# FFN coefficients broadcast in halves, the first during the second route, and half of F2's preparation in B's output path

## What is computed

```python
x = x + attn_a(layernorm(x))   # distances on a hyperboloid, 16 heads of 8
x = x + ffn(layernorm(x))      # "F1"
x = x + attn_b(layernorm(x))   # rotary softmax attention, 16 heads of 8; "B"
x = x + ffn(layernorm(x))      # "F2", the same weights as F1
```

```python
scores = sigmoid(x @ router_w.T)
sfc = scores + e_bias                      # choice only
group_scores = top_k(sfc by 8 groups, 2).sum   # best 4 groups stay
topk_idx = top_k(masked sfc, 8)
coef = scores of the chosen / their sum * 2.5, else 0    # (T, 64)
h = silu(x @ Wg[e]) * (x @ Wu[e]) * coef[:, e]           # all 64 experts
out = sum_e h @ Wd[e] + silu(x @ SWg) * (x @ SWu) @ SWd
```

## Time and profile before

| what | value |
|---|---|
| runs | 1180.27, 1181.67, 1187.24 us; median 1181.67 |
| profiled execution | 1185.19 us, span 1183.4 us |
| mean granted TensorE clock | 0.818 |
| PE busy | 982.2 us (83%), 5292 matmuls |
| DVE busy | 988.9 us (84%) |
| ACT, POOL busy | 693.6 us (59%), 343.4 us (29%) |
| DMA | 85.13 MB, mean 72 GB/s |
| F1's expert phase | about 392 to 666 us of the span |
| B | about 666 to 855 |
| F2's preparation and experts | about 855 to 1184 |

### The profile page before, as it was taken

How to read it: one execution, slowest core, us unless ns; L and a number is a source line. 1 busy time by engine, 2 the same in 40 slices (tenths; PEclk the granted TensorE clock), 3 DMA queues, 4 the chain that set the end, 5 groups by cost and what they waited for, 6 DMA issues and landing times.

```text
span 1183.4 us, 16824 instructions
## 1 busy us (share of the span) xinstructions
PE 982.2 (83%) x5292; PEld 712.1 (60%) x5292; DVE 988.9 (84%) x1489; ACT 693.6 (59%) x792; POOL 343.4 (29%) x215
## 2 busy tenths in 40 slices
PE   4774677766675899999999788999646999999997
PEld 3442344434443688888888546554534888888886
DVE  5649888888888699999999788996366999999996
ACT  2435999999994444455445451677253455445543
POOL 2003566555560142333332130100001333323320
PEclk8765555555556899999999895999957999999999
DMA  2000000000010697667663000000004987666651
GB/s 53 1 1 1 1 1 1 1 1 1 1 34 10 153 208 161 151 143 163 151 150 78 0 1 1 2 2 1 8 7 105 208 169 163 149 151 157 142 115 35
DMA packets 26236, 85.13 MB, mean 72 GB/s; under 512 B 3920, under 2 KB 17232, under 8 KB 18000
## 3 DMA queue, kind: packets, MB, share of 16 engines
q1 hardware_dynamic: 26192, 84.56, 32.1%
HBM read 82.45 MB, written 2.10 MB: 71 GB/s over the span
## 4 chain that ended last, share of the span: by engine, by line
PE 63%; DVE 22%; issue 9%; ACT 3%; DMA 2%; POOL 1%; SPq 0%; DVEq 0%; POOLq 0%; ACTq 0%
PE ps L445 60%; DVE xr L1682 4%; DVE xr L1674 3%; DVE mx L1824 3%; DVE stats L1442 1%; DVE rr L1690 1%; POOL rr L1344 1%; DVE hl L1915 1%; PE ps L507 1%; PE ps L832 1%; DMA cbc<-routing_coefficients 1%; DVE q L1853 1%; DVE mr L1585 1%; ACT f_xn L1172 1%; DMA routing_coefficients<-cT 0%
## 5 line engine op out<-in xcount | busy, mean ns | idle before, releaser
L1240 ACT ACTIVATE sg<-ps 128x512 f32<-128x512 f32 x264 | 156.8, 595 | 263.5 <-PE ps L445 263.5
L1908 DVE TENSOR_TENSOR hf<-sg,ps 128x512 f32<-128x512 f32 x264 | 172.6, 686 | 41.8 <-DVE hl L1915 23.6
L445 PE MATMUL ps<-xh,whi 128*128 128x512 f32 x528 | 206.3, 391 | 1.3 <-POOL wlo L1394 1.3
L445 PE MATMUL ps<-xh,wlo 128*128 128x512 f32 x528 | 205.5, 389 | 0.0
L445 PE MATMUL ps<-xl,whi 128*128 128x512 f32 x528 | 205.5, 389 | 0.0
L1344 POOL TENSOR_TENSOR rr<-xr,rr 128x2048 f32<-128x2048 f32 x32 | 144.9, 4546 | 193.3 <-ACT xr L1067 179.2
L1915 DVE TENSOR_TENSOR hl<-hf,hh 128x1024 fp32r<-128x1024 f32 x132 | 179.3, 1358 | 0.5 <-DVE hf L1908 0.5
L1392 POOL CAST whi<-wraw 128x384 fp32r<-128x384 f32 x66 | 53.9, 817 | 403.2 <-PE ps L445 267.4
L1920 DVE TENSOR_TENSOR hf<-hf,cbc 128x1024 f32<-128x1024 f32 x128 | 157.5, 1231 | 10.4 <-DMA cbc<-routing_coefficients 1.7
L1246 ACT ACTIVATE hh<-hf 128x1024 fp32r<-128x1024 f32 x132 | 139.0, 1053 | 5.0 <-DVE hf L1920 5.0
L1394 POOL TENSOR_TENSOR wlo<-wraw,whi 128x384 fp32r<-128x384 f32 x66 | 116.1, 1759 | 5.3
(11 more groups left out here) (251 smaller groups left out, 1597.1 us busy)
## 6 DMA issues: line engine op xcount, KB each, us to landing
cbc<-routing_coefficients SPq DMA_DIRECT2D x128, 512.0 KB, 6.3
wraw<-in_wexp_dram SPq DMA_DIRECT2D x66, 192.0 KB, 5.4
X<-in_x_dram SPq DMA_DIRECT2D x4, 256.0 KB, 4.5
routing_coefficients<-cT SPq DMA_DIRECT2D x8, 128.0 KB, 2.3
out_dram<-X SPq DMA_DIRECT2D x4, 256.0 KB, 2.9
rope_in<-in_consts_dram SPq DMA_DIRECT2D x1, 512.0 KB, 3.4
wa<-in_wA_dram SPq DMA_DIRECT2D x1, 256.0 KB, 3.8
w_in<-in_wB_dram SPq DMA_DIRECT2D x1, 128.0 KB, 3.2
```

The source lines that it names most:

```text
L445: return pe.matmul(o, l, r, start=start, stop=stop, **kw)
L1240: act.activation(sg[c % 2][:, :], bank(4 + 2 * (c % 2)), ACT.Silu).then_inc(s_sg, 1)
L1908: dve.tensor_tensor(hf[c // 2][:, c % 2 * FF_TOK:(c % 2 + 1) * FF_TOK], sg[c % 2][:, :], bank(5 + 2 * (c % 2)), ALU.mult).then_inc(s_h1, 1)
```

## The change

What it does:

- **SP.** A pair's coefficients are loaded in halves of 1024 tokens, with a semaphore per half. After the first half of the tokens is stored, the first halves of four pairs are loaded (eight transfers of 256 KB), before the second route's coefficients come; behind the second store the second halves of four pairs, with the weights of pairs 2 and 3 between. The shared weights and those of pairs 0 and 1 are loaded ahead of the first store, and POOL splits them without waiting for the barrier. The loop over pairs is one turn of four shorter and reloads each half as soon as it is used.
- **TensorE.** Behind the first half's transposed coefficients come chunks 0 and 1 of the shared expert and 24 zero matmuls into banks 0 and 2, then the second half's coefficients, which now go through banks 1 and 3, each of which is then started by a zero matmul. `meet(.., 2)` and `meet(.., 5)` are no barrier any more for TensorE, ScalarE, VectorE and POOL, and `meet(.., 4)` none for the first three.
- **B's output path** uses four banks instead of eight, and takes in the statistics of F2's groups 0 to 3, the normalisation, transposes and copies of groups 0 (ScalarE) and 1 (VectorE), and behind it their logits.
- The value tensor `vt` is kept for both attentions, so B's `b_vt` and its memset go. In F1 `marks()` stands a few instructions later.

The diff, cut to what changes the order:

```diff
...
@@ -378,39 +378,63 @@
             sp.dma_start(eb_s[:, :], brow[0:1, 2 * P:2 * P + E].broadcast_to([P, E])).then_inc(s_in, 16)
             sp.dma_start(rw_s[:, :], rwT).then_inc(s_in, 16)
+            def load_coefs(row0, s, side):
+                for e in range(2):
+                    row = c_d[bass.ds(row0 + e, 1), side * FF_PAIR:(side + 1) * FF_PAIR]
+                    sp.dma_start(cbc[s][e * I:(e + 1) * I, side * FF_PAIR:(side + 1) * FF_PAIR],
+                                 row.rearrange("a n -> (a n)").partition_broadcast(I)).then_inc(s_cl[side][s], 16)
+
+            def load_weights(pair, slot):
+                sp.dma_start(wraw[slot][:, :], wexp[bass.ds(pair, 1), :, :].rearrange("a p n -> p (a n)")
+                             ).then_inc(s_wl[slot], 16)
+
             def experts_phase(f):
                 base = (PAIRS + 1) * f
                 p0 = FF_PAIRS * f
-                with sp.Fori(0, PAIRS // 4) as i:
+                with sp.Fori(0, PAIRS // 4 - 1) as i:
                     for s in range(4):
-                        sp.wait_ge(s_ws, i * 4 + (base + s + CR_WS))
-                        sp.dma_start(wraw[s % 2][:, :], wexp[bass.ds(i * 4 + s, 1), :, :].rearrange("a p n -> p (a n)")
-                                     ).then_inc(s_wl[s % 2], 16)
-
-                        sp.wait_ge(s_h, i * 8 + (p0 + 2 * s - 4 + CR_H))
-                        for e in range(2):
-                            row = c_d[bass.ds(i * 8 + (2 * s + e), 1), :]
-                            sp.dma_start(cbc[s][e * I:(e + 1) * I, :],
-                                         row.rearrange("a n -> (a n)").partition_broadcast(I)).then_inc(s_cl[s], 16)
-
-            def store_coefs(f):
-                for i in range(GROUPS // 2):
-                    for g in range(2):
-                        sp.wait_ge(s_ch, lap(f, i, g) + CR_GRP)
-                        sp.dma_start(c_d[:, group(i, g)], cT[g][:, :]).then_inc(s_cst[g], 16)
+                        sp.wait_ge(s_ws, i * 4 + (base + s + 4 + CR_WS))
+                        load_weights(i * 4 + (s + 4), s % 2)
+                        for side in range(2):
+
+                            sp.wait_ge(s_h, i * 8 + (p0 + 2 * s + side + 3 + CR_H))
+                            load_coefs(i * 8 + (2 * s + 8), s, side)
+
+            def store_coefs(f, i):
                 for g in range(2):
-                    sp.wait_ge(s_cst[g], 2 * 16 * (f + 1) + CR_SCR)
-
-            def load_shared(f):
-
-                sp.dma_start(wraw[1][:, :], wexp[PAIRS]).then_inc(s_wl[1], 16)
+                    sp.wait_ge(s_ch, lap(f, i, g) + CR_GRP)
+                    sp.dma_start(c_d[:, group(i, g)], cT[g][:, :]).then_inc(s_cst[g], 16)
+                for g in range(2):
+                    sp.wait_ge(s_cst[g], 16 * (2 * f + i + 1) + CR_SCR)
+
+            def first_coefs(f):
+                base = (PAIRS + 1) * f
+                store_coefs(f, 0)
+                for s in range(4):
+                    load_coefs(2 * s, s, 0)
+                store_coefs(f, 1)
+                for s in range(4):
+                    load_coefs(2 * s, s, 1)
+                    if s in (1, 2):
+                        sp.wait_ge(s_ws, base + s + 1 + CR_WS)
+                        load_weights(s + 1, (s + 1) % 2)
+
+            def load_first(f):
+
+                sp.dma_start(wraw[0][:, :], wexp[PAIRS]).then_inc(s_wl[0], 16)
+
+            def load_second(f):
+
+                sp.wait_ge(s_ws, (PAIRS + 1) * f + 1 + CR_WS)
+                load_weights(0, 0)
+                load_weights(1, 1)
...
@@ -827,23 +853,23 @@
                     if half == 1:
                         pe.wait_ge(s_on, B + 2 * c + 1)
                     elif c >= 2:
-                        pe.wait_ge(s_on, B + 2 * c - 2)
+                        pe.wait_ge(s_ores, B + c - 1)
                     for r in range(8):
-                        last = pe.transpose(bank(4 * (c % 2) + r // 4)[:, r % 4 * P:(r % 4 + 1) * P],
+                        last = pe.transpose(bank(2 * (c % 2) + r // 4)[:, r % 4 * P:(r % 4 + 1) * P],
                                             o_all[:, c, :].rearrange("p (l r) -> p r l", r=16)[:, 8 * half + r, :],
                                             ident)
                     last.then_inc(s_oP, 1)
-                def projected(c):
+                def transposed(c):
                     pe.wait_ge(s_on, B + 2 * c + 2)
                     for j in range(4):
-                        last = pe.transpose(bank(4 * (c % 2) + 2)[:, j * P:(j + 1) * P], b_otok[c % 2][:, j, :], ident)
+                        last = pe.transpose(bank(2 * (c % 2))[:, j * P:(j + 1) * P], b_otok[c % 2][:, j, :], ident)
                     last.then_inc(s_oT, 1)
+
+                def projected(c):
                     pe.wait_ge(s_oTs, B + c + 1)
-                    if c >= 2:
-                        pe.wait_ge(s_ores, B + c - 1)
                     for j in range(4):
-                        last = mm(bank(4 * (c % 2) + 3)[:, j * P:(j + 1) * P], b_oT[c % 2][:, j * P:(j + 1) * P],
+                        last = mm(bank(2 * (c % 2) + 1)[:, j * P:(j + 1) * P], b_oT[c % 2][:, j * P:(j + 1) * P],
                                   wo_b[:, :])
                     last.then_inc(s_wo, 1)
@@ -851,24 +877,30 @@
                 for c in range(CHUNKS):
                     token_major(c, 0)
                     if c >= 1:
+                        transposed(c - 1)
                         projected(c - 1)
                     token_major(c, 1)
+                f_transposed(1, 0, 0)
+                transposed(CHUNKS - 1)
+                f_transposed(1, 0, 1)
                 projected(CHUNKS - 1)
-
-            def spare(i, g):
-
-                return 4 * i + 2 * g
+                for g in range(2):
+                    logits(1, 0, g)
+
+            def spare(f, i, g):
+
...
             def prepare_f(f):
                 if f == 0:
                     pe.wait_ge(s_oTs, B)
                 else:
-                    for g in range(2):
-                        f_transposed(f, 0, g)
-                    for g in range(2):
-                        logits(f, 0, g)
+                    pe.wait_ge(s_ores, B + CHUNKS)
                 for g in range(2):
                     f_transposed(f, 1, g)
                 if f == 0:
                     pe.wait_ge(s_ores, B)
                 for g in range(2):
                     logits(f, 1, g)
+                if f == 1:
+                    pe.wait_ge(s_sc, lap(f, 1, 1))
                 coefs_transposed(f, 0)
                 if f == 0:
                     rope_tables()
+                    pe.wait_ge(s_natc, 1)
+                pe.wait_ge(s_sc, lap(f, 1, 1))
+                pe.wait_ge(s_xh, lap(f, 1, 1))
+                pe.wait_ge(s_xl, FF_STEPS * f + 2)
+                pe.wait_ge(s_ws, (PAIRS + 1) * f + 1 + CR_WS)
+                for c in range(2):
+                    gate_up((PAIRS + 1) * FF_STEPS * f + c, 3, c, True)
+                pe.wait_ge(s_z, f + 1)
+                for k in range(24):
+                    mm(bank(2 * (k % 2)), zr[:, 0:P], zr[:, :], start=True, stop=False, skip_group_check=True)
+                pe.wait_ge(s_ch, lap(f, 0, 1) + CR_GRP)
                 coefs_transposed(f, 1)
-
-                pe.wait_ge(s_z, f + 1)
-                pe.wait_ge(s_ch, lap(f, 0, 1) + CR_GRP)
-                if f == 0:
-                    pe.wait_ge(s_natc, 1)
-                for c in range(FF_STEPS):
-                    mm(bank(c), zr[:, 0:P], zr[:, :], start=True, stop=False, skip_group_check=True)
+                for g in range(2):
...
@@ -1155,35 +1194,47 @@
             def o_of_b():
                 for c in range(CHUNKS):
                     act.wait_ge(s_oT, B + c + 1)
-                    act.activation(b_oT[c % 2][:, :], bank(4 * (c % 2) + 2), ACT.Copy).then_inc(s_oTs, 1)
-
-            def spare(i, g):
-
-                return 4 * i + 2 * g
+                    act.activation(b_oT[c % 2][:, :], bank(2 * (c % 2)), ACT.Copy).then_inc(s_oTs, 1)
+                    if c == 1:
+                        f_norm_std(1, 0)
+                    elif c == 2:
+                        f_norm_apply_group(1, 0)
+                        f_norm_std(1, 1)
+                        f_norm_copy_group(1, 0, 0)
+
...
@@ -1217,27 +1274,23 @@
                     act.wait_ge(s_xh, 2)
                     f_norm_copy(f, 1)
                 else:
-                    for g in range(GROUPS):
+                    f_norm_copy_group(f, 0, 1)
+                    for g in range(2, GROUPS):
                         f_norm_std(f, g)
-                    f_norm_apply(f, 0)
-                    f_norm_copy(f, 0)
+                    scores(f, 0)
+                    act.wait_ge(s_fxn, GROUPS + 2)
                     f_norm_apply(f, 1)
-                    scores(f, 0)
                     f_norm_copy(f, 1)
                 scores(f, 1)
                 coef_copies(f, 0)
```

(19 more changed lines are left out.)

153 lines of the change are left out of this document (82 added, 71 removed).

## The result

The changed kernel takes 1177.61 us (median of 20 runs, 1171.25 to 1201.18). The kernel before takes 1198.14 (20 runs, 1180.27 to 1218.67); the three of them that I knew, median 1181.67, were among its quickest. The ratio is 0.9895, with an interval of 0.9863 to 0.9927; it leaves out every run more than 1.5% above the fastest of its kernel, which cuts the kernel before off near 1198. My 1161.0 was 16.6 too low.

The account below looks back on a forecast made before the run. TensorE was taken as full in both expert phases, gains only at their entries. 11.6 - 1.0 + 4.1 + 1.6 + 3.4 + 1.3 - 0.3 = 20.7 us off 1185.2 gave 1164.5, 1161.0 as median; range 1155 to 1170.

Parts of the forecast that it names:

- Part 1: B's output path: takes in half of F2's preparation, so the second route starts at 859.5 instead of 871.1, 11.6 us gained.
- Rival C: B's output path: engine hand-overs delay the last residual, half of the 11.6 us is lost, 1167 us; chance 13%.
- Part 2: Second route of each expert entry: shared chunks and zero matmuls gain 3.4 us (after -0.4) first, 4.1 second, nothing lost there.
- Rival A: Both entries: clock does not rise or stay with zero matmuls, 12.5 us lost instead of 0.4, 1173 us; chance 5%.
- Part 3: Expert phases: weights and first coefficient halves fetched early remove waits, gaining 1.3 us in the first and 1.6 in the second.
- Rival B: Start of both expert phases: second coefficient halves land late, VectorE waits up to 3 us, 1167 us; chance 12%.
- Rival D: Expert loop: a half-row transfer costs as much as a whole, +118 us over 56 pairs, 1279 us; chance 3%.
- no bound: Expert loop: SP issues four half-row transfers per pair in under 3 us of an 8.2 us pair, so no bound.
- Part 4: Routes: POOL's weight splits hold up VectorE on the shared port, costing 1.0 us in the second entry, 0.3 in the first.
- a: Stretch from the first route's end (second coef) to the last y of F1: 276.6 us before, forecast 271.9.
- c: Stretch from B's last residual to the second route's end (second coef): 41.7 us before, forecast 30.4.
- d: Stretch from the second route's end (second coef) to the last y of F2: 278.9 us before, forecast 273.2.

Follow-up runs that it names:

- experiment 3: Changed kernel with 14 zero matmuls in the first entry and 37 in the second instead of 24 each: 1179.25 us, ratio 0.9839.
- experiment 7: Kernel before plus a second VectorE wait per pair: 8.143 us per pair (before 8.113), 1194.93 us; changed early-row kernel, wait moved to ScalarE: 8.113, 1169.47, repeated 1166.31.
- the row in B: 16 full-array filler matmuls at B's third pair of shifted steps, added to the changed kernel with fitted zeros and fillers before last y: 1167.53 us; wait on ScalarE too: 1166.31.
- experiments 3 and 4: Experiment 3, and the changed kernel with filler matmuls at the end of B's preparation and in the first 13 score tiles: 1185.62 us.

## Why the prediction was wrong

**The step that failed** is one I did not write down: that what lies between the two entries keeps its time. I costed B at +0.7. B's length is set by how long TensorE's clock is at 0.50 in the samples, a quarter of that time being lost, and this is 37.6 us in the profile I had, 37.6 again in one other trace of it and 54.6 to 92.2 in three more of the same or nearly the same kernel, 71.7 in the profile of the changed one. The earlier trace rows ended at 431 to 660.8 and began again at 856.2; the stretch between went into no term. It cost 7.1 of the missing 14 us in the profile. It also goes with the other half of the miss, the base: in the runs of the kernel before, time and mean clock go together, and the median of three that I started from, 1181.67, was 16.5 us lower than the median of all 20 (1198.14). From that median my 20.7 would have given 1177.4, next to the measured 1177.61, but by luck: B's clock gave part of that difference, and the terms below were off. The line PEclk of the page of the kernel before held the warning: slice 25 of 40 is a 5 inside B, with TensorE busy 8 tenths of it. So did a wide table by stretch of the same trace, with 0.76 and 0.92 inside B.

```profile
PE   4774677766675899999999788999646999999997
...
PEclk8765555555556899999999895999957999999999
```
```profile
670.00:725.00 55.00, 45.08 (x185) 25.68 (x185) 44.91 (x87) 22.78 (x39) 11.32 (x12) 0.76 0.00 1
725.00:835.00 110.00, 102.36 (x1034) 55.97 (x1034) 85.94 (x155) 72.99 (x80) 4.53 (x1) 0.92 0.01 1
```

**Part 1** (11.6): right. 15.8 to 3.66 us is 12.1, the last residual comes 0.56 later (its step took 4.86 instead of 4.30; I had 0.7). Rival C is out in the profile: none of it was lost.

**Part 2**: the way from `coef` to the third chunk was right where the chip was as assumed, and mis-sized by what stood ahead of it. First entry, -0.4: the rope copies ended 1.7 late at half clock and the zero matmuls 2.0 behind `coef` instead of 0.4. Second entry, "nothing lost": TensorE went idle for 3.38 us and the experts began at 0.50, 1.5 us (experiment 3). Rival A was not it: all 24 zero matmuls of either entry ran 0.227 us apart at 1.00. The Trainium skill (TensorE: Matmul & The Clock Gate, What's actually happening) says that activity releases the clock and idleness throttles it, and names no exception for zeros. The zeros here agree, at 1.00 throughout, and so do the idle 3.38 us, in which the clock fell.

**Part 3** (1.3, 1.6): right in its mechanism: no wait for `wlo` or `cbc`, TensorE 3.0 to 3.3 us ahead from the third pair on, where the 4.7 forecast for the first phase less the 1.6 of the late zeros is 3.1. Rival B (halves late) did not happen: a half landed in 3.8 us, at most 7.9, and none kept VectorE waiting. Rival D fell too, DMA share 0.50 in the loop where it was 0.62. What I called no bound had another price: VectorE's second wait, 0.8 us in each phase (experiment 7). I looked at SP's cost of four transfers and never at the wait that they brought to VectorE. The last y of F1, mostly at 0.50, took another 1.6 (4.21 us instead of 2.63 from its first matmul to its last).

**Part 4** (-1.0, -0.3): -1.6 and -0.3. The first half of the second route took 14.0 us from `sfc` to `coef` beside POOL's three `wlo`, and 12.4 in the kernel with the front undone, where they run ahead of it. Three instructions make up the 1.6: `sfc` took 0.95 us (above) where it takes 0.69 alone, and these two 1.10 and 1.37 where they take 0.42 and 0.69:

```profile
867.03 1.10 DVE L1611 TENSOR_TENSOR top<-sfc 128x256 f32<-128x256 f32 x1
872.80 1.37 DVE L1633 TENSOR_TENSOR mk<-sfc,gm 128x512 f32<-128x512 f32 x1
```

In the first entry one was held up (`sfc`, 1.38 at 359.14), and the first route ended 0.3 later (389.20 for 388.94).

**What the terms come to.** Mended (fitting zeros, fillers ahead of the last y, wait on ScalarE) the stretches are a 271.5, c 31.4, d 272.4 against a forecast of 271.9, 30.4, 273.2. So the mechanisms of the four parts are there, but their sizes are reached only with three edits, one of which (the fillers ahead of the last y) also takes away 1.2 us that the kernel before loses at 0.50 in F2's last y. With the row in B that kernel takes 1166.3, 1.3% less than the prediction's base of three runs; its ratio to the kernel before is 0.9754.

## What to carry to other kernels

Before a sum is made from a profile, read the clock of every stretch, also of those that the change does not touch: a long stretch at 0.50 with TensorE busy can differ from one execution of the same kernel to the next, and three quick runs don't show how often it comes. Compare kernels stretch by stretch between named events, and repeat the kernel before. Matmuls meant to bridge a wait should end with it: too many delay what follows, too few let the clock fall in front of the work they were to protect. And count every wait that a finer transfer adds to an engine at 93%.

## What the runs showed of the hardware

- TensorE 96 and 99% busy stayed at the 1.2 GHz level for 160.4 and for 64.9 us (experiments 3 and 4). All but 48 of the 1073 matmuls there, and all but 24 of the 488, used a quarter of the array, 32 rows by 128 columns or 128 rows by 32 columns. A row of 16 matmuls over the full array and 512 columns was followed by 2.4 GHz 2.4 to 5.4 us after its start in nine of nine traces (744.8, 744.3 and 731.3 are three of the starts). The Trainium skill (TensorE: Matmul & The Clock Gate, What's actually happening) has the clock set by how busy TensorE has been lately. Busy time as the profile counts it does not tell these two kinds of work apart; the clock does.
- The clock also fell at 737.9 and 740.9, with TensorE 96 and 100% busy in the 10.9 us before, 1.4 and 1.1 us after the start of the last filler, when only such thin matmuls followed.
- A wait that had long been fulfilled, once more per pair on VectorE, cost TensorE 0.033 us per pair of experts, and none when ScalarE had it. By which way is open.
